# First stage of a fused attention kernel: queries ahead of keys, loads on two queues in order of use, null rows added later

## What is computed

```python
xn = layernorm(x);  q = xn @ Wq;  k, v = split(context @ Wkv)
k = concat(null_key, k);  v = concat(null_value, v)   # one extra row per head
q, k = tanh(q), tanh(k)
attn = softmax(q k^T / 8)
x = x + (attn v) @ Wout + bout
```

## Time and profile before

| | us |
|---|---|
| median of three runs | 217.09 |
| the three runs | 215.47, 217.09, 217.73 |
| profiled execution | 214.31 |
| its span, first to last instruction | 212.5 |
| PE / DVE / ACT / POOL busy | 195.8 / 146.0 / 120.6 / 39.1 |

### The profile page before, as it was taken

One profiled execution on the slowest core, in us unless ns is written; L12 is line 12 of the kernel. 1 busy time (PEld: TensorE's weight loads), 2 busy tenths in 40 slices (PEclk: granted clock), 3 DMA queues, 4 the chain that ended last, 5 costly groups with the idle time before them and its releaser, 6 DMA issues.

```text
span 212.5 us, 4137 instructions
## 1 busy us (share of the span) xinstructions
PE 195.8 (92%) x1627; PEld 146.2 (69%) x1629; DVE 146.0 (69%) x249; ACT 120.6 (57%) x221; POOL 39.1 (18%) x40
## 2 busy tenths in 40 slices
PE   6895679999999999999999999999988899999991
PEld 1793578898988889888988877956755334635560
DVE  3459798889788799998988869833873737124313
ACT  3197678788888888878888864004631123331300
POOL 4139202204022040220311700020401400000001
PEclk9999999999999999999999999999999999999999
DMA  5896669971102011010000695999999400000000
GB/s 170 286 390 173 144 191 349 369 199 51 52 2 97 3 49 52 0 52 0 2 3 0 232 386 176 324 382 377 378 377 377 160 0 0 3 0 0 3 0 28
DMA packets 22853, 31.02 MB, mean 146 GB/s; under 512 B 1953, under 2 KB 18866, under 8 KB 22834
## 3 DMA queue, kind: packets, MB, share of 16 engines
q1 hardware_dynamic: 22834, 30.76, 43.2%
HBM read 29.57 MB, written 0.13 MB: 140 GB/s over the span
## 4 chain that ended last, share of the span: by engine, by line
PE 53%; issue 21%; DVE 13%; ACT 4%; DMA 3%; POOL 2%; SPq 1%; POOLq 0%; DVEq 0%
PE ps L1008 34%; PE ps L1042 6%; DVE keys L734 5%; DMA w_k_stage<-in_Wkv 3%; PE ps L1082 2%; PE ps L1096 2%; DVE ex_l L700 2%; PE ps L1188 1%; DVE mixT L744 1%; PE ps L996 1%; DVE q_split L725 1%; PE ps L1069 1%; PE ps L1172 1%; PE ps L1227 1%; DVE ex_sum L755 1%
## 5 line engine op out<-in xcount | busy, mean ns | idle before, releaser
L734 DVE SCALAR_TENSOR_TENSOR keys<-ps,keys 64x512 f16<-64x512 f32 x64 | 44.1, 689 | 7.1 <-ACT keys L573 5.7
L1008 PE MATMUL ps<-ctxT_h,w_k_h 128*128 128x256 f32 x128 | 39.4, 308 | 2.5 <-DVE keys L734 2.1
L573 ACT ACTIVATE keys<-ps 64x512 f16<-64x512 f32 x64 | 37.8, 591 | 1.8
L1008 PE MATMUL ps<-ctxT_h,w_k_l 128*128 128x256 f32 x128 | 36.6, 286 | 0.0
L1008 PE MATMUL ps<-ctxT_l,w_k_h 128*128 128x256 f32 x128 | 36.6, 286 | 0.0
L1008 PEld LDWEIGHTS ps<-ctxT_h,w_k_h 128*128 128x128 f32 x128 | 24.8, 194 | 4.2 <-issue 3.0
L569 ACT ACTIVATE ps<-ps 128x512 f32<-128x512 f32 x32 | 18.6, 582 | 14.7 <-PE ps L1008 14.7
L700 DVE TENSOR_TENSOR ex_l<-ps,ex_h 128x512 fp32r<-128x512 f32 x32 | 22.1, 691 | 6.7 <-ACT ps L603 6.1
L1008 PE MATMUL ps<-ex_h,ctx_h 128*128 128x512 f32 x64 | 25.7, 401 | 0.0
L1008 PE MATMUL ps<-ex_l,ctx_h 128*128 128x512 f32 x64 | 25.3, 395 | 0.0
L1008 PEld LDWEIGHTS ps<-ctxT_l,w_k_h 128*128 128x128 f32 x128 | 25.0, 195 | 0.0
(11 more groups left out here) (175 smaller groups left out, 260.2 us busy)
## 6 DMA issues: line engine op xcount, KB each, us to landing
w<-in_fc1T SPq DMA_DIRECT2D x8, 1024.0 KB, 12.3
w<-in_fc SPq DMA_DIRECT2D x8, 1024.0 KB, 11.9
stage_t<-in_ctxT SPq DMA_DIRECT2D x8, 256.0 KB, 5.0
stage_n<-in_ctx SPq DMA_DIRECT2D x8, 256.0 KB, 4.6
w_k_stage<-in_Wkv SPq DMA_DIRECT2D x4, 256.0 KB, 6.2
mixT<-in_Wq SPq DMA_DIRECT2D x2, 512.0 KB, 6.2
q_two<-q_split SPq DMA_DIRECT2D x8, 128.0 KB, 4.0
w_v<-in_Wkv SPq DMA_DIRECT2D x1, 1024.0 KB, 5.4
```

Of the source, the lines that this page charges most:

```text
L573: nc.scalar.activation(keys[rows, u % 2, PK * i:PK * (i + 1), r], full[rows].rearrange("p (j n) -> p j n", j=PK), ACT.Copy, scale=UNIT).th ...
L734: V.scalar_tensor_tensor(out=keys[other, u % 2, PK * i:PK * (i + 1), r], in0=ps[mine, K_BANK + kp % 2].rearrange("p (j n) -> p j n", j=PK) ...
L1008: last = MM(dst, lhs[i], rhs[j], start=start and m == 0, stop=stop and m == len(parts) - 1)
```

## The change

The order of the first stage is written anew.

- **PE**: 12 warm-up matmuls ahead of the transposes. Then queries of the first half of the heads, keys 0, keys 1, queries of the second half, keys 2. The two matmuls with the null key go behind the scores of steps 0 and 1.
- **Loads**: ACT's queue now issues ctxT 0, `w_k` 0, `w_k` 1, the second half of `w_q` and `w_k` 2; SP's issues x, the identity alone, the first half of `w_q`, the null key, `w_k` 3, ctx 0, ctxT 1, the first four of `q_two`, ctx 1, the other four, ctxT 2, ctx 2, ctxT 3, and only then constants, small vectors, `w_v`, `w_out` and the rest.
- **ACT**: its table load is moved between its issues. It makes the high parts of `w_k` 0 and 1 alone.
- **DVE**: it makes the high parts of ctxT 0 and of `w_k` 2 and 3, and no low part of `w_k`. ctxT n + 2 is cast two steps earlier in the loop. The sum of a step is added in the step itself.
- **POOL**: it clears `ex_sum` at the very start and makes all four low parts of `w_k`. The null rows of batch 1 are copied early, those of batch 0 are added when the sums of batch 0 are whole (step 16); the denominators wait for them.

```diff
-            load_wk(0)
-            load_ctxT(0)
...
-            load_wk(1)
+            sp.dma_start(const[:, 0:C_ONES], a["const"][:, 0:C_ONES]).then_inc(ld_eye, 16)
+            sp.dma_start(w_q_half(w_q, 0), w_q_half(chunked("Wq"), 0)).then_inc(ld_wq[0], 16)
             sp.dma_start(null_k[:], a["null_k"]).then_inc(ld_null, 16)
-            sp.dma_start(null_v[:], a["null_v"]).then_inc(ld_null_v, 16)
-            load_wk(2)
-            load_wk(3)
+            sp.dma_start(w_k_piece(w_k_stage, 3), w_k_source(3)).then_inc(ld_wk[3], 16)
             load_ctx(0)
             load_ctxT(1)
+            spread_queries(0)
             load_ctx(1)
+            spread_queries(1)
+            load_ctxT(2)
+            load_ctx(2)
+            load_ctxT(3)
...
+            load_ctx(3)
+            sp.dma_start(w_v[:], a["Wkv"][:, INNER:2 * INNER].rearrange("(c p) n -> p c n", p=P)).then_inc(ld_wv, 16)
+            sp.dma_start(w_out[:], chunked("Wout")).then_inc(ld_wv, 16)
+            load_ctxT(4)
...
+            nc.gpsimd.memset(ex_sum[:], 0.0).then_inc(zero_ready, 1)
             pool.wait_ge(half_ready, 1)
...
-                    low_wk(2)
-                    low_wk(3)
+                    for i in range(G * KT):
+                        low_wk(i)
                     low_ctxT(1)
...
+                        if i == NC:
+                            pool.wait_ge(esum_ready, STEPS // B)
+                            pool.wait_ge(ctxT_ready, i + 1)
+                            for r in range(2):
+                                sums, mine = null_rows(0, r)
+                                nc.gpsimd.tensor_tensor(sums, sums, mine, ALU.add).then_inc(null_sums, 1)
...
+            act.dma_start(stage_t[:, 0], ctxT_source(0)).then_inc(ld_ctxT[0], 16)
+            load_wk(0)
+            act.preload_act_table_set("exp_and_others")
+            load_wk(1)
+            act.dma_start(w_q_half(w_q, 1), w_q_half(chunked("Wq"), 1)).then_inc(ld_wq[1], 16)
+            load_wk(2)
             split_wk(0)
-            act.wait_ge(ld_ctxT[0], 16)
-            copy(ctxT_h[:, 0], stage_t[:, 0], first_high)
             split_wk(1)
             act.wait_ge(ld_null, 16)
             nc.scalar.activation(null_kt[:], null_k[:], ACT.Tanh).then_inc(nk_tanh, 1)
+            queries_tanh(0)
             keys_tanh(0)
...
             keys_tanh(1)
+            queries_tanh(1)
             keys_tanh(2)
...
+                if s < G:
+                    null_exp(s)
...
             norm_stats(0, x0[:])
+            dve.wait_ge(ld_ctxT[0], 16)
+            V.tensor_copy(ctxT_h[:, 0], stage_t[:, 0]).then_inc(first_high, 1)
             normalise(0, xn[:], x0[:]).then_inc(xn_ready, 1)
-            split_wk(0)
...
-            split_wk(1)
             split_queries(0)
+            high_wk(2)
+            low_keys(0)
+            high_wk(3)
+            low_keys(1)
+            split_queries(1)
             high_ctxT(1)
-            low_keys(0)
-            split_queries(1)
-            low_keys(1)
             high_ctx(0)
+            low_keys(2)
...
-                if t == KT - 1 and g == G - 1 and n + 2 < B * NC:
+                if t == KT - 1 and g == 0 and n + 2 < B * NC:
                     high_ctxT(n + 2)
...
-            warm(8, 7)
+            warm(12, 7)
             pe.wait_ge(ld_eye, 16)
             transpose_xn(0)
             warm(2, 7)
+            queries(0)
             project_keys(0)
...
             project_keys(1)
+            queries(1)
             project_keys(2)
             LAG = 2
             for s in range(STEPS):
-                if s == LAG:
-                    pe.wait_ge(null_ready, 2)
+                if s in (LAG, LAG + KT):
+                    pe.wait_ge(null_ready, (s - LAG) // KT + 1)
                 scores(s)
+                if s < G:
+                    null_scores(s)
```

More of the change, by code:

```diff
@@ L368, in w_k_piece, with chunked, w_k_source, ctxT_source @@
             return w[:, i // KT, :, (i % KT) * PK * P:(i % KT + 1) * PK * P]
+        def chunked(name, p=P):
+            return a[name].rearrange("(c p) n -> p c n", p=p)
+        def w_k_source(i):
+            return chunked("Wkv")[:, :, i * PK * P:(i + 1) * PK * P]
+        def ctxT_source(n):
+            return chunked("ctxT")[:, :, n * CK:(n + 1) * CK]
+        def ctx_source(n):
+            return a["ctx"][n * CK:(n + 1) * CK].rearrange("(t p) d -> p t d", p=P)
+        def w_q_half(w, half):
+            return w[:, :, half * 512:(half + 1) * 512]
         block = whole.enter_context(nc.Block())
@@ L375, in load_ctxT @@
             def load_ctxT(n):
[L376 to L383, removed]
+                if n == 2:
+                    sp.wait_ge(first_ready, 1)
+                elif n > 2:
+                    sp.wait_ge(ctxT_ready, n - 2)
+                sp.dma_start(stage_t[:, n % 2], ctxT_source(n)).then_inc(ld_ctxT[n], 16)
             def load_ctx(n):
@@ L388, in load_ctx @@
                     sp.wait_ge(ctx_ready, n - 1)
[L389 to L397, removed]
+                sp.dma_start(stage_n[:, n % 2], ctx_source(n)).then_inc(ld_ctx[n], 16)
             def in_each_row(name):
                 return a[name].rearrange("(o d) -> o d", o=1).broadcast_to([P, a[name].shape[0]])
[L402 to L422 removed]
             def spread_queries(g):
@@ L437, in _ @@
                              a["b2"][e:e + 1, :].broadcast_to([SLOTS, D])).then_inc(ld_small, 16)
[L438 to L441, removed]
+            load_ctx(4)
             sp.dma_start(w_lq[:], chunked("lWq")).then_inc(ld_lin, 16)
@@ L449, in _ @@
             sp.dma_start(w_route[:], chunked("wg")).then_inc(ld_lin, 16)
-            for n in range(3, B * NC):
+            for n in range(5, B * NC):
                 load_ctxT(n)
@@ L492, in low_ctx, with null_rows @@
                 low_part(ctx_l[:, n % 2], stage_n[:, n % 2], ctx_h[:, n % 2]).then_inc(ctx_ready, 1)
+            def null_rows(b, r):
+                row = slice(64 * r, 64 * r + 1)
+                sums = ex_sum[row].rearrange("p (j r) b q -> p r b j q", r=2)[:, r, b]
+                return sums, null_ex[row].rearrange("p j (b q) -> p b j q", b=B)[:, b]
             for n in range(3):
@@ L1065, in denominators @@
                 pe.wait_ge(esum_ready, STEPS - (G - 1 - g) * KT)
+                pe.wait_ge(null_sums, 4)
+                pe.wait_ge(ld_const, 16)
                 for j in range(PG):
@@ L1098, in output, with queries, null_scores @@
                     last.then_inc(wo_psum, 1)
+            def queries(g):
+                pe.wait_ge(xnT_ready, 1)
+                pe.wait_ge(ld_wq[g], 16)
+                for j in range(PG * g, PG * (g + 1)):
+                    for c in range(DC):
+                        last = MM(ps[:, 1 + g, (j % PG) * P:(j % PG + 1) * P], w_q[:, c, j * P:(j + 1) * P],
+                                  xnT[:, c], start=c == 0, stop=c == DC - 1)
+                last.then_inc(q_psum, 1)
+            def null_scores(g):
+                pe.wait_ge(q_tanh, g + 1)
+                pe.wait_ge(nk_tanh, 1)
+                MM(ps[:, NULL_BANK[g]], null_kt[:], qT[:, PG * g:PG * (g + 1)].rearrange("p j t -> p (j t)"), start=True,
+                   stop=True).then_inc(null_psum, 1)
             pe.wait_ge(warmer_ready, 1)
-            warm(8, 7)
+            warm(12, 7)
             pe.wait_ge(ld_eye, 16)
```

99 lines of the change are left out of this document (51 added, 48 removed).

## The result

| | before | changed |
|---|---|---|
| median, us | 216.28 (4 runs: 215.34 to 217.73) | 209.10 (4 runs: 208.14 to 211.59) |
| profiled execution | 214.31 | 208.19 |
| its span | 212.5 | 206.1 |

The account below looks back on a forecast made before the run. The prediction took the attention loop to be bound by PE, so the time moves with the loop's start. Gains of 4.6 us there and 0.4 in the loop made 217.09 - 5.0 = 212.1, forecast as 212.0, range 209.4 to 215.0.

Parts of the forecast that it names:

- the sum at the end: Whole kernel: 4.6 + 0.4 = 5.0 us gained, taken from the median 217.09 to give 212.1, forecast as 212.0.
- T: Start of the scores of step 2 in the attention loop: 28.73 us before, forecast at 24.1.
- The bound: Attention loop: bound by PE, with 100.82 us of work in 101.27, so all that follows moves with the loop.
- The start: First stage: xn ready near 5.1 us, warm-ups end and transposes start at 6.5 to 6.7, fast clock before the first queries.
- The slower rival: DVE's cast of ctxT 2 in step 1 waits for a late load and holds later keys; 220 possible; chance 0.05.
- The full-rate rival: Start loads: two filled queues run at 350 GB/s from the third microsecond, time 210.0; chance 0.12.
- Term one: Start of the scores of step 2: 24.1 for 28.73 us, from two chains, a gain of 4.6 us.
- chain two: Queries and PE ahead of step 2: q_two takes 6.6 or 4.8 us, so step 2 starts at 23.3 to 25.1.
- Term two: Attention loop: earlier casting of ctxT removes PE's 0.42 us idle at 94.22, a gain of 0.4 us.
- Term three: Median 217.09 against profiled execution 214.31: the 2.8 us between them taken as lying outside the kernel's work.

Follow-up runs that it names:

- e2: Kernel before with only the cast of the next ctxT on DVE moved two steps earlier, loads as they were: 222.07 us, ratio 1.0265.
- e3: Changed kernel with all loads of the start issued from SP's one queue, in order of use: 207.51 us, ratio 0.9632.
- e13: Kernel before, unaltered, run and profiled again: 216.22 us, ratio 1.0018.
- e10: Kernel before with only 12 warm-up matmuls and ex_sum cleared at the start: 216.30 us, ratio 0.9987.
- e14: Kernel before with 8 more warm-up matmuls behind keys 2, where PE idles ahead of the scores of step 0: 216.31 us, ratio 0.9973.
- e6: Changed kernel with the null rows handled as in the kernel before, null matmuls and exponentials ahead of keys 2: 213.29 us, ratio 0.9845.
- e12: Changed kernel, one load queue, w_q half ahead of w_k 0, first queries' tanh earlier, w_k 0's low part on DVE, 6 warm-ups behind transposes: 208.20 us, ratio 0.9617.
- e15: Changed kernel with all start loads on SP's queue and 6 warm-up matmuls for 2 behind the transposes: 207.82 us, ratio 0.9583.
- e11: Kernel before with only its loads put in order of use, on its one queue: 213.66 us, ratio 0.9867.
- e1: Changed kernel, unaltered, run and profiled again: 208.26 us, ratio 0.967.
- e8: Changed kernel with the cast of the next ctxT on DVE two steps later again, as before: 209.07 us, ratio 0.9687.
- e4: Changed kernel with 8 warm-up matmuls for 12: 210.42 us, ratio 0.9742.

## Why the prediction was wrong

**The step that failed** is the sum at the end, in three of its terms. It gave 217.09 - 5.0 = 212.1 where 209.10 was measured, 3.0 us less. T was put 1.0 us too late, the loop's gain 0.4 too small, and the 2.8 us between the profiled execution and the median, taken as lying outside the kernel's work and so as unchanged, shrank to 0.9 (209.10 - 208.19), 1.9 less. Against that, the changed kernel has 2.1 us outside its span for 1.8, 0.3 more, for which no cause is known. The mechanism of the first two terms was right and their sizes off; the third was a wrong reading, and it is the largest.

**What held.** The bound: behind T the loop is PE's, the tail follows it unchanged (83.2 and 83.3 us from the last denominators). The start: transposes at 6.15 for 6.5, and `xn` (5.8 for 5.1) of no use to PE. `w_k` 0, 1 and 2 at 6.7, 8.9 and at most 12.6, where 7.5, 9.2 and 13.0 stood. Scores of step 0 at 17.0, just below the 17.4 to 19.2 that stood. `q_low` at 12.65, where 12.6 stood, is luck: the queries came later (w_q at 8.68 for 7.5), and DVE's scaling did not meet POOL's low part, which was over at 10.87. The slower rival, the load in front of DVE's cast, has its mechanism (e2), not its place here. The full-rate rival's 210.0 lies nearest to the result, but not by its cause: the loads moved 181 GB/s over the first 6 us, and 316 and 354 only from 6 to 9 and 9 to 12 us.

**Term one: T, 24.1 for 23.12, worth 1.0 us.** Two chains were given, 23.6 by DVE and 23.3 to 25.1 by the queries, and the middle was taken. DVE's was the right one in kind, 0.5 too late: from low keys 0 to T it was given 10.1 us and took 9.58, because its casts and scalings were to wait behind POOL (at 1.57 per piece, for 1.26 to 1.30) and fell between POOL's pieces instead. Its start was right by luck: 13.5 was taken from the landing of `w_k` 2, which DVE did not wait for; what released low keys 0 at 13.54 was ACT's tanh of keys 0, behind w_q, the first queries and keys 0. The other 0.5 came from chain two. Its upper end was `q_two` at 6.6 us from its first issue to its last landing, a number from a trace in which the constants and vectors stood ahead of it; the change moves those behind. Scores of step 0 started 4.3 us after the first issue, when `low_keys` 1 was done; where `q_two` itself was awaited (e3) it took 4.2. The lower end of 4.8 was the row that fits better. A chain through w_q's landing and then queries, keys 0 and 1, queries, keys 2 and ACT, which is as long as DVE's, was not added up.

**Term two: the loop, 0.4 for 0.83.** I read the idle column (0.42 at 94.22) and took it for the price. The step there is 3.98 us long (93.16 to 97.14) and one at 38.86 is 3.60, for 3.38: 0.60 and 0.22. The ends of pipelined matmuls are modelled in these timelines, the idle column counts from them, and the first of these two gaps has no entry there at all. Starts of a line that repeats are the measure.

**Term three: the 2.8 us between the profiled execution and the median, put outside the kernel's work.** That was wrong. The profiled execution of before (214.31) is below every other of its runs. In e13, e10 and e14 the spans differ from 212.5 by 0.9, 2.5 and 1.7 us, and step 6 starts later by 0.95, 2.5 and 1.8: the whole of it lies in the first 45 us. In these profiles it has two sources: the clock that falls in the 2.3 us of idle PE ahead of step 0, and the landing of ctxT 2, which varies between 37.6 and 40.2 behind the 2.5 MB of `b`, `w_v` and `w_out`. The change removes both the stretch and the late issue, which fits the 1.9 us; that the runs without a profile lose time in the same two places is not shown. In return the change has an idle stretch of its own, 1.1 to 2.1 us ahead of the queries, where the prediction had "no gap from 1.31 on" although its own landing of w_q lay behind the end of the warm-ups. In some executions the queries then start at the slow level (e6, 3.65 us), which is where single runs 2 us above the rest may come from, as e12 and e15 suggest by filling that stretch; no profile of such a run of the changed kernel itself was had.

**Which part of the change brings it.** The order of the loads alone 2.5 to 2.9 us (e11), warm-ups and early clearing alone nothing (e10), the cast alone a loss of 5.8 (e2). Taken out of the changed kernel, by the medians: null rows 4.7 (between profiles with a like clock at the start 2.5 at T and 4.0 by step 6), keys first 3.1, warm-ups 2.2, the cast 0.5 (1.4 in its profile), the second queue nothing. These do not add up to 7.2, and should not: several chains end within a microsecond of each other, so the last that is mended gets the whole gain.

## What to carry to other kernels

When a stage has several chains of nearly one length, undoing a part tells what it is worth in company and doing it alone tells what it is worth by itself; here the four warm-up matmuls are 2.2 us and nothing. A view of the chain that ended last shows one chain; look whether another engine works without a gap beside it. An idle stretch of PE costs its own length and, in some executions, the clock behind it, so look at the granted clock of the stretch behind each one in more than one profile before taking a profiled time as the kernel's. Price a gap of a periodic loop by the distance of starts, not by the idle column.

## What was not expected of the hardware

- The same idle stretch of PE, 2.33 and 2.34 us, left the granted clock at 1.00 in one execution and at 0.66 over the 5 us from 22 to 27 in another of the same kernel.
- Two queues filled from two engines loaded no sooner than one: the first half of `w_q` at 8.02 to 8.86 us in five profiles from two (changed, e1, e8, e4, e6), at 8.04 and 7.98 from one (e3, e15).
- The granted clock at the start can mislead: in the profile of before it stands at 1.00 from the first microsecond on the earlier trace rows, also where 12 matmuls take 2.77 us for 1.52, while e4 and e14 show 0.50 and 0.57 where their matmuls are slow. Set the pace of the matmuls beside it.
- After the same 8 warm-up matmuls, the first 12 projection matmuls of the same kernel took 2.77 us in one execution and 1.52 in another (e13).
- A POOL subtraction of 128x512 takes 1.26 to 1.30 us alone and 1.72 where it meets DVE's split of the queries (e12). Beside low keys, which read `ps`, it takes 1.28 (changed, from 13.07), and DVE's price stays at 1.41.
